# Attention heads of a macaron block: who rounds and who subtracts when probabilities are split in two parts

## The reference, cut to what matters

```python
q, k, v = x @ Wq.T, x @ Wk.T, x @ Wv.T      # 16 query heads, 4 key/value heads of 32
q, k = rope(q), rope(k)
scores = einsum('bhqd,bhkd->bhqk', q, repeat(k, 4)) * 32 ** -0.5
attn = softmax(scores, axis=-1)
out = einsum('bhqk,bhkd->bhqd', attn, repeat(v, 4)) @ Wo.T
x = x + out
```

## Time and profile before

| what | value |
|---|---|
| median of the runs shown | 1814.27 us (3 runs, 1813.62 to 1815.49) |
| time of the profiled execution | 1809.72 us |
| its span, first to last instruction | 1807.7 us |
| granted TensorE clock, mean | 0.974 |
| busy: PE matmul | 1684.5 us (93%) |
| busy: VectorE (DVE) | 1078.8 us (60%) |
| busy: ScalarE (ACT) | 864.4 us (48%) |
| busy: GpSimd (POOL) | 974.3 us (54%) |
| VectorE row maxima L1799 | 256, mean 1213 ns |
| ScalarE exp L1487 | 256, mean 1014 ns |

### The profile page before, as it was taken

One profiled execution on the slowest core, in us unless ns is written; L12 is line 12 of the kernel. 1 busy time (PEld: TensorE's weight loads), 2 busy tenths in 40 slices (PEclk: granted clock), 3 DMA queues, 4 the chain that ended last, 5 costly groups with the idle time before them and its releaser, 6 DMA issues.

```text
span 1807.7 us, 25091 instructions
## 1 busy us (share of the span) xinstructions
PE 1684.5 (93%) x8596; PEld 1344.3 (74%) x8596; DVE 1078.8 (60%) x1846; ACT 864.4 (48%) x1274; POOL 974.3 (54%) x727
## 2 busy tenths in 40 slices
PE   6999999999977989999999999877799999999997
PEld 5888898999866756666666666545688889999985
DVE  4554322222687879999999999995445432222226
ACT  4322232322324359999999998872323122322320
POOL 3115673336522148989898988840030619550745
PEclk9999999999988989999999999998989999999999
DMA  9205543333630000000000000003010535432427
GB/s 333 97 24 218 207 175 131 120 132 120 193 134 1 1 2 1 1 2 1 1 1 2 1 1 2 13 13 142 1 53 1 222 122 196 161 140 84 167 86 240
DMA packets 54310, 160.01 MB, mean 89 GB/s; under 512 B 6704, under 2 KB 7600, under 8 KB 51632
## 3 DMA queue, kind: packets, MB, share of 16 engines
q1 hardware_dynamic: 41360, 84.74, 13.3%
q0 software_dynamic: 12832, 73.67, 11.4%
HBM read 102.29 MB, written 55.84 MB: 87 GB/s over the span
## 4 chain that ended last, share of the span: by engine, by line
PE 60%; DVE 15%; ACT 12%; issue 6%; DMA 6%; POOL 1%; SPq 0%; ACTq 0%; POOLq 0%; DVEq 0%
PE PS L1021 11%; PE PS L1023 10%; PE PS L1022 10%; ACT PT L1487 5%; DVE nmf L1799 4%; PE PS L1217 4%; DMA xn<-x_routed 3%; ACT Ph L1494 3%; DMA xs<-x_routed 2%; PE PS L1143 2%; PE PS L1148 2%; PE PS L1146 2%; PE PS L1145 2%; PE PS L1147 2%; PE PS L1144 2%
## 5 line engine op out<-in xcount | busy, mean ns | idle before, releaser
L1956 POOL TENSOR_TENSOR Pl<-PT,Ph 128x1024 fp32r<-128x1024 f32 x176 | 433.4, 2475 | 86.4 <-ACT Ph L1494 81.4
L1799 DVE TENSOR_REDUCE nmf<-PS 128x1 f32<-128x1024 f32 x256 | 307.8, 1213 | 30.6 <-PE PS L1217 30.4
L1487 ACT ACTIVATE PT<-PS 128x1024 f32<-128x1024 f32 x256 | 259.5, 1014 | 23.7 <-PE PS L1235 17.0
L1250 PE MATMUL PS<-Ph,V 128*65 128x512 f32 x512 | 205.5, 401 | 13.5 <-DVE Pl L1822 12.7
L1494 ACT ACTIVATE Ph<-PT 128x1024 fp32r<-128x1024 f32 x184 | 194.9, 1059 | 35.0 <-PE PS L1251 32.6
L1251 PE MATMUL PS<-Pl,V 128*65 128x512 f32 x512 | 202.1, 395 | 0.0
L1871 POOL TENSOR_TENSOR W<-raw,W 128x544 fp32r<-128x544 f32 x144 | 190.1, 1355 | 1.5
L1217 PE MATMUL PS<-KS,QS 96*128 96x512 f32 x512 | 171.5, 416 | 19.0 <-ACT PT L1487 13.2
L1774 DVE TENSOR_TENSOR thid<-thid,PS 128x352 f32<-128x352 f32 x78 | 40.7, 521 | 245.8 <-ACT thid L1413 245.8
L1235 PE MATMUL PS<-QS,KS 98*128 98x512 f32 x512 | 173.2, 420 | 3.0 <-DVE nmf L1799 2.9
L1413 ACT ACTIVATE thid<-PS 128x352 f32<-128x352 f32 x78 | 36.2, 464 | 260.4 <-PE PS L1148 260.4
(11 more groups left out here) (183 smaller groups left out, 4107.9 us busy)
## 6 DMA issues: line engine op xcount, KB each, us to landing
raw<-ffn_w POOLq DMA_DIRECT2D x18, 2176.0 KB, 10.2
y_routed<-ytile SPq DMA_DIRECT2D x78, 256.0 KB, 2.1
xn<-x_routed SPq DMA_DIRECT2D x40, 256.0 KB, 2.8
x_routed<-xq SPq DMA_DIRECT2D x1, 9984.0 KB, 28.5
xs<-x_routed SPq DMA_DIRECT2D x38, 256.0 KB, 4.0
raw<-ffn_w SPq DMA_DIRECT2D x6, 768.0 KB, 10.6
raw<-ffn_w SPq DMA_DIRECT2D x2, 2176.0 KB, 9.2
x_home<-X SPq DMA_DIRECT2D x4, 1024.0 KB, 5.8
```

Source lines behind the costliest of these rows:

```text
L1250: e.matmul(PS[0:VCOL, ob, :], V[:, b * QT + kt, g, :], Ph[:, u % PBUF, js], start=kt == 0, stop=False)
L1487: e.activation(PT[:, u % PTBUF, :], PS[:, i:i + 2, :].rearrange("p b n -> p (b n)"), ACT.Exp, scale=SCALE).then_inc(p_ready.sem, 1)
L1799: e.tensor_reduce(nmf[:, (n % 3) * REP + h, t:t + 1], PS[:, i:i + 2, :].rearrange("p b n -> p (b n)"), AX.X, ALU.max, negate=True).then_in ...
L1956: e.tensor_tensor(Pl[:, u % PBUF, :], PT[:, u % PTBUF, :], Ph[:, u % PBUF, :], ALU.subtract).then_inc(pl_pool.sem, 1)
```

## The change

`hi_on_vector` goes. `lo_on_vector` now also says who makes the high part. In the first seven head groups the units with u % 8 of 1, 4 and 6 have their high part copied by GpSimd and their low part subtracted by VectorE; the other five in eight have the high part from ScalarE and the low part from GpSimd. In the last group the units with u % 4 of 1, 2 and 3 go to GpSimd and VectorE, and those with u % 4 == 0 to ScalarE and GpSimd. VectorE makes no high part any more. In all: 148 high parts on ScalarE, 108 on GpSimd; 148 low parts on GpSimd, 108 on VectorE.

VectorE's low part of unit u − 1 also moves in the list: from behind the row maximum of step u to the head of step u + 1, ahead of `scores` of u + 1, and so on VectorE's queue behind `store_head` of step u and ahead of the next row maximum.

```diff
--- before.py
+++ after.py
@@ -184,12 +184,9 @@
     return n, un // QT, un // (QT // 2) % 2, un % (QT // 2)
 
 
-def hi_on_vector(u):
-    return u % 4 == 1 or u // UNITS == len(KV_GROUPS) - 1 and u % 4 == 3
-
-
 def lo_on_vector(u):
-    return u % 4 == 2 or u // UNITS == len(KV_GROUPS) - 1 and u % 4 != 0
+
+    return u % 4 != 0 if u // UNITS == len(KV_GROUPS) - 1 else u % 8 in (1, 4, 6)
 
 
 def beside_heads(n):
@@ -399,6 +396,8 @@
             work.append(("split_hi", in_flight[-1]))
             if not lo_on_vector(in_flight[-1]):
                 work.append(("split_lo", in_flight[-1]))
+        if len(in_flight) > 1 and lo_on_vector(in_flight[-2]):
+            work.append(("split_lo", in_flight[-2]))
         work.append(("scores", u))
         in_flight.append(u)
         if lows:
@@ -410,8 +409,6 @@
             work.append(("place_max", *lows[-1]))
         if n + 1 < groups and un % QT == QT - 1:
             maxima.append((n + 1, un // QT))
-        if len(in_flight) > 1 and lo_on_vector(in_flight[-2]):
-            work.append(("split_lo", in_flight[-2]))
         if in_flight[0] == u - LAG:
             w = in_flight.pop(0)
             work.append(("values", w))
@@ -647,8 +645,8 @@
 
     max_done, max_taken, max_turned, max_hi, max_ready = (
         signal(n) for n in ("max_done", "max_taken", "max_turned", "max_hi", "max_ready"))
-    s_done, p_ready, ph_act, ph_dve, pl_dve, pl_pool, pv_done = (
-        signal(n) for n in ("s_done", "p_ready", "ph_act", "ph_dve", "pl_dve", "pl_pool", "pv_done"))
+    s_done, p_ready, ph_act, ph_pool, pl_dve, pl_pool, pv_done = (
+        signal(n) for n in ("s_done", "p_ready", "ph_act", "ph_pool", "pl_dve", "pl_pool", "pv_done"))
     ot_ready, ot_turned, head_ready = (signal(n) for n in ("ot_ready", "ot_turned", "head_ready"))
     o_done, o_added = signal("o_done"), signal("o_added")
 
@@ -812,7 +810,7 @@
             s_done.plan(*key)
             p_ready.plan(*key)
         elif kind == "split_hi":
-            (ph_dve if hi_on_vector(*key) else ph_act).plan(*key)
+            (ph_pool if lo_on_vector(*key) else ph_act).plan(*key)
         elif kind == "split_lo":
             (pl_dve if lo_on_vector(*key) else pl_pool).plan(*key)
         elif kind == "values":
@@ -1486,7 +1484,7 @@
                     act.wait_ge(pl_dve if lo_on_vector(u - PTBUF) else pl_pool, u - PTBUF)
                 e.activation(PT[:, u % PTBUF, :], PS[:, i:i + 2, :].rearrange("p b n -> p (b n)"),
                              ACT.Exp, scale=SCALE).then_inc(p_ready.sem, 1)
-            elif kind == "split_hi" and not hi_on_vector(*key):
+            elif kind == "split_hi" and not lo_on_vector(*key):
                 u, = key
                 act.wait_ge(p_ready, u)
                 if u >= PBUF:
@@ -1808,15 +1806,9 @@
                 dve.wait_ge(q_ready, PROJECTED[-1])
                 for g in range(NG):
                     dve.wait_ge(home_out[g])
-            elif kind == "split_hi" and hi_on_vector(*key):
-                u, = key
-                dve.wait_ge(p_ready, u)
-                if u >= PBUF:
-                    dve.wait_ge(pv_done, u - PBUF)
-                e.tensor_copy(Ph[:, u % PBUF, :], PT[:, u % PTBUF, :]).then_inc(ph_dve.sem, 1)
             elif kind == "split_lo" and lo_on_vector(*key):
                 u, = key
-                dve.wait_ge(ph_dve if hi_on_vector(u) else ph_act, u)
+                dve.wait_ge(ph_pool, u)
                 if u >= PBUF:
                     dve.wait_ge(pv_done, u - PBUF)
                 e.tensor_tensor(Pl[:, u % PBUF, :], PT[:, u % PTBUF, :], Ph[:, u % PBUF, :],
@@ -1948,9 +1940,15 @@
                     pool.wait_ge(home_out[g])
                 pool.wait_ge(max_taken, 0, REP - 1, QT - 1)
                 pool.wait_ge(max_turned, 0, REP - 1)
+            elif kind == "split_hi" and lo_on_vector(*key):
+                u, = key
+                pool.wait_ge(p_ready, u)
+                if u >= PBUF:
+                    pool.wait_ge(pv_done, u - PBUF)
+                e.tensor_copy(Ph[:, u % PBUF, :], PT[:, u % PTBUF, :]).then_inc(ph_pool.sem, 1)
             elif kind == "split_lo" and not lo_on_vector(*key):
                 u, = key
-                pool.wait_ge(ph_dve if hi_on_vector(u) else ph_act, u)
+                pool.wait_ge(ph_act, u)
                 if u >= PBUF:
                     pool.wait_ge(pv_done, u - PBUF)
                 e.tensor_tensor(Pl[:, u % PBUF, :], PT[:, u % PTBUF, :], Ph[:, u % PBUF, :],
```

## The result

The changed kernel takes 1962.19 us (median of 4 runs, 1961.41 to 1970.3) against 1813.94 us for the kernel before beside it (4 runs, 1813.36 to 1815.49): ratio 1.0826, 95% interval 1.0797 to 1.0855. The forecast was 1841 with 1824 to 1880: the direction was right, the size was not, +148 us instead of +27. The profiled span is 1959.6 us (before 1807.7), the mean granted TensorE clock 0.930 (before 0.974).

A forecast was written before the change was run, and what follows sets the result against it. It took one resource shared by GpSimd and VectorE, held by one at a time and full, to bound the heads stage. +18.5 us (groups 1 to 7) and +8.8 us (last group) made 1814.3 + 27 = 1841 us, range 1824 to 1880.

The forecast's parts named there:

- The sum ... is the whole period: Groups 1 to 7: shared-resource times 4.63 + 0.55 + 0.32 + 2.34 + 1.09 = 8.93 us fill the period of four units.
- The five terms: Four units' GpSimd and VectorE operations on the shared resource, end to end: 4.63, 0.55, 0.32, 2.34 and 1.09 us.
- the ScalarE–PE loop: Groups 1 to 7: ScalarE and PE waiting on each other, said to be not far behind the shared resource.
- c: Price of the new GpSimd copy of 128x1024 on the shared resource: 1.00 us, with ends 0.92 and 1.20.
- Rival 4: GpSimd copy as dear as a GpSimd subtraction, 2.33 us, in all groups: about 1985 us; chance 3%.
- The sum for groups 1 to 7: Shared-resource time removed and added: net +0.66 us per eight units, x 28 = +18.5 us.
- The moved step, costed at nothing: VectorE's subtraction at the next step's head, groups 1 to 7: waits of at most 2.33 us, taken as covered, cost nothing.
- a mean wait up to (18.45 − 14.0) / 3 = 1.47 us: VectorE's spare time over eight units, spread on three subtractions: a mean wait up to 1.47 us is covered.
- The last group: Last 32 units: shared resource becomes the bound, 18.9 us for eight units instead of 16.7, +8.8 us.
- rival 1: VectorE, caught behind GpSimd's subtractions, becomes the bound: +38 us beyond forecast in groups 1 to 7, about 1879 us; chance 17%.
- Rival 2: Heads stage: loop of ScalarE and PE is the real bound, ScalarE's relief counts: −30 us, about 1785 us; chance 10%.

The follow-up runs named there:

- b_half_sub: Kernel before, GpSimd's subtraction cut from 1024 to 512 columns in one unit of eight (u % 8 == 3, groups 1 to 7): 1808.86 us, ratio 0.9977.
- b_third: Kernel before, with a third low part in eight (unit 4) moved from GpSimd to VectorE: 1826.33 us, ratio 0.9998.
- a_memset_160: Changed kernel plus a GpSimd memset of 160 columns behind each GpSimd copy of groups 1 to 7: 1874.57 us, ratio 1.0268.
- a_26: Changed kernel, old order, groups 1 to 7's GpSimd copies and VectorE low parts only for u % 8 of 2 and 6: 1964.74 us, ratio 1.0751.
- a_halves: Changed kernel with each GpSimd subtraction of 1024 columns made as two of 512: 1953.03 us, ratio 1.0677.
- a_246: Changed kernel, old order, with units u % 8 of 2, 4, 6 in place of 1, 4, 6: 1867.72 us, ratio 1.0226.

## Why the prediction was wrong

**What bounds the kernel: wrong.** "The sum ... is the whole period" was true and proved nothing. The resource was busy or handed over all the time in the one stretch that I added up, but b_half_sub and b_third took 1 us out of it and the period stayed: GpSimd's starts are set by others, and its instructions fill the time they are given. The five terms were taken from one end to the next, so they had to add up to the period; what they did show is that no term held a gap. A full ledger shows that a resource could be the bound; only taking work away shows that it is. I did write that the ScalarE–PE loop wasn't far behind; the chain before says that it is ahead, with no GpSimd instruction in it from 700 to 1100 us.

**Prices: right.** The GpSimd copy alone took 1.026 us at the least and 1.037 in the median, and the next GpSimd instruction starts 0.98 to 1.00 us behind it; c was 1.00. Rival 4 is out. The page's 1.8 cycles an element (the Trainium skill, "GPSIMD Engine Reference", "Elementwise — side-by-side cycle accounting") would be an estimated 1.54 us; the trace goes with the other price.

**The sum for groups 1 to 7: near what the kernel without the tie takes.** It said 18.45 us for eight units. With the tie broken, a_memset_160 has 901.19 to 920.61, 19.42 us, of which the three memsets are 0.6: 18.8. Against 17.9 this is +0.9 x 28 = 25 us, where the sum has +18.5. GpSimd is busy or kept out by VectorE there in all but 0.6 us, but that is a full ledger again, and no run took work out of it: that the sum comes near for its own reason isn't shown, and it may be luck.

**The moved step, costed at nothing: the step that failed.** Three things in it.
- "What is queued behind it on VectorE is the next row maximum" left out `place_low`, which for one low part in eight is next in the list, and for which PE's turn, and all of PE's queue behind it, stand. The list in the code would have shown it.
- "The mean over random arrivals in a subtraction would be 2.33 / 2 = 1.17". The arrival isn't random. The low part is released by the end of a GpSimd instruction, which is just when the next GpSimd instruction begins, and that one was first, mostly by 0.06 to 0.08 us: the wait is the whole subtraction, 3.35 − 1.09 = 2.26 us, in nearly every long case, and 7.3 us in a_26.
- The cover of "a mean wait up to (18.45 − 14.0) / 3 = 1.47 us" compared VectorE's total work with the period. PE doesn't wait for a mean but for one instruction: the mean low part in the changed kernel is 1904 to 1978 ns, a mean wait of 0.8 to 0.9 us over the 1.09 of the sum, well inside the cover, and 3.4 us were lost each time.

**The clock wasn't in the sum.** Behind a PE stall of 3.42 us stand 13 matmuls at the 1.2 GHz level, 2.67 us more. It nearly doubled the price: 6.1 us x 23.

**The last group: right.** The forecast was 18.9 us for eight units instead of 16.7, +8.8 us. GpSimd's Wo copies now stand at 1323.22 and 1341.54, 18.3 us apart: + 1.6 x 4 = +6.4 us.

```profile
1323.22 1.60 POOL L1959 CAST Wo<-woraw 128x512 fp32r<-128x512 f32 x1
...
1341.54 1.60 POOL L1959 CAST Wo<-woraw 128x512 fp32r<-128x512 f32 x1
```

**The rivals.** What happened is rival 1's mechanism, VectorE caught behind GpSimd's subtractions, given 17% and +38 us beyond the forecast: right in kind, wrong in where it bites (one seat, not the mean) and in price (it lacked the seat's 23 stalls and the clock). Of what the profile "would show" for it, a mean above 2.3 us isn't there, and PE waits little for row maxima (8.4 us) and 76.3 us for `place_low`. Rival 2's premise, that the pair of engines isn't the bound, is borne out by b_half_sub and b_third, and its loop of ScalarE and PE by the chain before. Its time was not: the stalls behind VectorE came on top, and no run here shows what the relief of ScalarE alone is worth.

## What to carry to other kernels

When an instruction is moved or released anew, write down the instruction next in its engine's queue and who waits for that one, and price the worst single case, not the mean: an in-order queue passes on the longest wait. When two engines exclude each other and one releases the other, the releaser's own next instruction, if it is ready, is there first; put something harmless, or something that doesn't exclude, between the two (letting a third engine give the release wasn't tried here). And before a full resource is called the bound, see whether the chain that ended last runs through it, and take one piece of work out of it on the chip.

## What the runs showed of the hardware

- **Losing a tie.** A VectorE subtraction issued 0.06 to 0.08 us behind a GpSimd subtraction of 1024 columns waited it out, and where GpSimd had more queued, that went ahead too: one instruction more at 4.38 us, three more at 8.41 us. One issued 0.78 us into a subtraction got in at the next handover (2.68 us). The Trainium skill, "SBUF — State Buffer", "SBUF: two separate sides", says that whoever starts first has the port pair for the whole instruction and the other fully blocks; the trace agrees for the first instruction. Who is next after it isn't settled by these runs: in a_halves, 0.08 us behind a first half of 512 columns, VectorE got in behind that half 18 times and behind both 10 times, and in a_246 one that was issued 0.08 us into the short stack subtraction (902.79) was held up by that alone.

```profile
902.87 1.47 DVE L1813 TENSOR_TENSOR Pl<-PT,Ph 128x1024 fp32r<-128x1024 f32 x1 [1.02 <-POOL Ph L1947]
```

- **A GpSimd memset isn't kept out.** It runs beside VectorE's subtraction (memset 903.62, 0.52 us; VectorE from 903.71, 1.23 us), and neither is longer for it.
- **The clock after a stall.** After 3.42 us without a matmul PE started 13 matmuls 0.43 us apart; after 2.63 us (a_halves, matmul at 915.26) the granted clock was 0.57 over the next 3 us; after 1.29 us (a_memset_160) no matmul was slow, with 1.00 over the next 5 us.
